# Expert outputs summed into the tokens' rows in memory, tile by tile, in a decoder block's sparse expert stage

## The reference

```python
xb = x + cross_attention(...)            # "after_cross"
x1 = self_attention(norm(xb)) + xn       # "x1"
h  = rmsnorm(x1) * ln2
s  = sigmoid(h @ router_w)               # 8 experts
top2 = argtop2(s + router_bias)          # ties: the lower expert
w  = s[top2] / sum(s[top2])              # the two shares
y  = sum over the two: w_e * ((silu(h @ wg[e]) * (h @ wu[e])) @ wd[e])
out = xb + x1 + y
```

## Time and profile before

| | us |
|---|---|
| median of 3 runs (3554.36 to 3559.09) | 3554.7 |
| the profiled execution | 3556.26 |
| its span, first to last instruction | 3554.5 |
| PE, DVE, ACT, POOL busy in the span | 3236.8, 2161.2, 1898.1, 1598.7 |
| granted TensorE clock, mean | 0.966 |
| expert block, from 3209.4 | 345.1 |

### The profile page before, as it was taken

The page is one execution under the profiler, slowest core; times in us unless marked ns, Lnnn a source line. Parts: engine busy times, 40 slices in busy tenths (PEclk is TensorE's granted clock), DMA queues, the critical chain, the costliest instruction groups (busy, mean ns, idle before and its releaser), DMA issues. The chain is left out here.

```text
span 3554.5 us, 61087 instructions
## 1 busy us (share of the span) xinstructions
PE 3236.8 (91%) x19346; PEld 2592.7 (73%) x19346; DVE 2161.2 (61%) x4705; ACT 1898.1 (53%) x4656; POOL 1598.7 (45%) x3082
## 2 busy tenths in 40 slices
PE   6799999999999999999899789799979999994992
PEld 3688888888888888888788455588857777772441
DVE  5476767677767676767553688654455756752223
ACT  3567676777676767676421477544353635531110
POOL 2677777777777777777330010255531010102103
PEclk8799999999999999999999899999989999997996
DMA  4122222222222222222342344333342021208325
GB/s 115 54 62 73 58 66 64 72 60 74 61 61 64 71 64 70 66 70 63 111 149 70 134 146 147 128 114 100 107 166 79 28 97 48 72 19 292 119 89 163
DMA packets 439368, 325.54 MB, mean 92 GB/s; under 512 B 131057, under 2 KB 348401, under 8 KB 438033
## 3 DMA queue, kind: packets, MB, share of 16 engines
q1 hardware_dynamic: 434064, 306.75, 29.0%
q0 software_dynamic: 5120, 16.78, 1.5%
HBM read 190.43 MB, written 133.04 MB: 91 GB/s over the span
## 5 line engine op out<-in xcount | busy, mean ns | idle before, releaser
L634 PE MATMUL gd_PJ<-xn_lead,gd_w_rest 128*128 128x512 f32 x1024 | 421.6, 412 | 0.0
L634 PE MATMUL gd_PJ<-xn_lead,gd_w_lead 128*128 128x512 f32 x1024 | 403.3, 394 | 0.0
L634 PE MATMUL gd_PJ<-xn_rest,gd_w_lead 128*128 128x512 f32 x1024 | 401.8, 392 | 0.0
L1076 POOL TENSOR_TENSOR gd_T<-gd_T,gd_prod 32x14 f32<-32x14 f32 (+6 forms) x896 | 312.5, 349 | 70.2
L1073 POOL TENSOR_TENSOR gd_prod<-gd_L,gd_T 32x14 f32<-32x14 f32 (+6 forms) x896 | 285.2, 318 | 70.2
L799 DVE SCALAR_TENSOR_TENSOR gd_conv<-gd_pre,gd_cur_a,gd_conv 128x512 f32<-128x512 f32 x384 | 300.5, 783 | 9.3 <-ACT gd_conv L957 2.4
L634 PEld LDWEIGHTS gd_PJ<-xn_lead,gd_w_lead 128*128 128x128 f32 x1024 | 193.6, 189 | 43.7
L634 PEld LDWEIGHTS gd_PJ<-xn_lead,gd_w_rest 128*128 128x128 f32 x1024 | 194.4, 190 | 37.4
L634 PEld LDWEIGHTS gd_PJ<-xn_rest,gd_w_lead 128*128 128x128 f32 x1024 | 194.6, 190 | 35.2
L2486 ACT ACTIVATE sa_E<-sa_B,sa_nmax 128x512 f32<-128x512 f32 (+3 forms) x256 | 131.4, 525 | 130.5 <-DVE sa_nmax L2602 130.5
L932 DVE SCALAR_TENSOR_TENSOR gd_og<-gd_B,ptab,gd_gate 128x512 f32<-128x512 f32 x64 | 48.0, 751 | 248.1 <-PE gd_B L648 248.1
(11 more groups left out here) (449 smaller groups left out, 8861.7 us busy)
## 6 DMA issues: line engine op xcount, KB each, us to landing
expert_rows<-xt_blank SPq DMA_DIRECT2D x16, 2048.0 KB, 7.5
turned_queries_keys<-f_wq SPq DMA_DIRECT2D x16, 1280.0 KB, 6.0
x_wo<-decay_sums SPq DMA_DIRECT2D x64, 256.0 KB, 3.9
triangles<-gd_Lo SPq DMA_DIRECT2D x64, 256.0 KB, 3.5
gd_W<-turned_image SPq DMA_DIRECT2D x64, 256.0 KB, 2.9
gd_T<-inverse_image SPq DMA_DIRECT2D x64, 256.0 KB, 3.4
gated_outputs<-gd_og SPq DMA_DIRECT2D x64, 256.0 KB, 2.8
go_ogt<-gated_outputs SPq DMA_DIRECT2D x16, 1024.0 KB, 5.9
```

The lines of the kernel that those rows point to most:

```text
L634: mm = pe.matmul(bank, w_parts[wp][:, j, k, :], rhs, start=(k == 0 and wp == 1), stop=(k == KT - 1 and wp + xp == 0))
L1076: nc.gpsimd.tensor_tensor(T16[:, rows, 0:j], T16[:, rows, 0:j], prod[:, rows, 0:j], ALU.subtract).then_inc(solving, 1)
```

## The change

Every row that travels to an expert gets 16 more floats (rows of 2112 bytes): the token's number, its first choice and its two shares. Behind the 16384 rows, 128 more are cleared, and all cleared rows carry numbers of 128 spare rows of the output sums. The shares are worked out with the routing (`shares`, eight small DVE operations on a batch), one step h after the second pick, and picks, places and rows come one to two steps h earlier than before.

A new memory tensor `sums` takes xb + x1. For batches 0 to 2 this is done in the middle of the next batch's heads: SP loads `after_cross` tiles into the two `hT` buffers, POOL adds them to `x1` in place, SP stores the result, and only then loads the next residual. For the last batch it is done in the expert block: SP issues four loads of `after_cross` behind the weights and ahead of the first expert tile, POOL adds, SP stores. The store of `x1` at each batch's end, the reload of `x1` and of all of `after_cross`, `slots`, the gathers, the additions of the last part and the 16 stores to `out` are gone.

In the expert loop DVE works out each tile's weight from what came with its rows (`weigh`, three small operations), ACT scales `y` by it on the way out of PSUM, and POOL adds the tile into `sums` by an indirect DMA that accumulates. POOL issues the one for tile j only when that for tile j - 1 has landed. `xr` has six buffers; SP reloads one when the accumulation of the tile in it has landed. After the last accumulation SP copies `sums` to `out`, memory to memory, in four transfers of 1 MB. The core of the diff:

```diff
-            slots()
-            shares()
+            shares(nc, then, R, last)
@@ self_attention, SP
+                    load_base(r, 0)
+                    load_base(r, 1)
+                    for i in range(CH):
+                        sp.wait_ge(base_added, r * CH + i + 1)
+                        sp.dma_start(acc_dram[bass.ds(r * SEQ + i * P, P), :], xt[:, i, :]).then_inc(R.base_out, 16)
+                        if i + 2 < CH:
+                            load_base(r, i + 2)
+                    sp.wait_ge(R.base_out, (r + 1) * CH * 16)
+                    load_residual(b)
-                for i in range(CH):
-                    sp.wait_ge(x1_ready, b * CH + i + 1 + CH)
-                    sp.dma_start(x1_dram[bass.ds(b * SEQ + i * P, P), :], xt[:, i, :]).then_inc(R.x1_out, 16)
@@ moe_sparse, SP
+            for i in range(CH):
+                sp.dma_start(xb[:, i, :], xb_dram[(last * CH + i) * P:(last * CH + i + 1) * P, :]).then_inc(xb_in, 16)
             load(0)
             load(1)
+            for i in range(CH):
+                sp.wait_ge(base_added, i + 1)
+                sp.dma_start(acc_dram[(last * CH + i) * P:(last * CH + i + 1) * P, :], R.x1[:, i, :]).then_inc(R.base_out, 16)
+            for j in range(2, MT):
+                sp.wait_ge(xr_turned, j - 1)
+                load(j)                                           # from j = 6: also summed >= 16 * (j - 5)
+            sp.wait_ge(summed, 16 * MT)
+            for b in range(B):
+                sp.dma_start(out_dram[b * SEQ:(b + 1) * SEQ, :], acc_dram[b * SEQ:(b + 1) * SEQ, :]).then_inc(out_done, 16)
@@ moe_sparse, POOL
+            pool.wait_ge(xb_in, 16 * CH)
+            for i in range(CH):
+                nc.gpsimd.tensor_tensor(R.x1[:, i, :], R.x1[:, i, :], xb[:, i, :], ALU.add).then_inc(base_added, 1)
+            pool.wait_ge(R.base_out, 16 * TILES)
+            for j in range(MT):
+                if j > 0:
+                    pool.wait_ge(summed, 16 * j)
+                pool.wait_ge(y_ready, j + 1)
+                rows = xr[:, j % SLOTS, AT_ID:AT_ID + 1].bitcast(I32)
+                nc.gpsimd.indirect_dma_start(acc_dram, bass.IndirectOffsetOnAxis(rows, 0), y[:, j % 2, :], None, compute_op=ALU.add).then_inc(summed, 16)
@@ moe_sparse, ACT, move_out(j)
+                act.wait_ge(weighted, j + 1)
                 if j >= 2:
-                    act.wait_ge(y_out[j % 2], j // 2 * 16)
-                nc.scalar.copy(y[:, j % 2, :], psY[j % 2][:, :]).then_inc(y_ready, 1)
+                    act.wait_ge(summed, 16 * (j - 1))
+                nc.scalar.activation(y[:, j % 2, :], psY[j % 2][:, :], ACT.Copy, scale=weight[:, j:j + 1]).then_inc(y_ready, 1)
@@ moe_sparse, DVE, between the gate product of tile j and the turned product of tile j - 1
+                weigh(j)
```

More of the change, by code:

```diff
@@ L2241, in drop_expert, with shares @@
     then(nc.vector.tensor_tensor(R.key[:], R.key[:], R.eq[:], ALU.add))
+def shares(nc, then, R, r):
+    for turn in range(2):
+        then(nc.vector.tensor_tensor(R.eq[:], R.pick[:, turn, R.tiles(r), :], R.sig[:, R.tiles(r), :], ALU.mult))
+        then(nc.vector.tensor_reduce(R.row[:, turn, :], R.eq[:], AX.X, ALU.add))
+    then(nc.vector.tensor_tensor(R.total[:, :], R.row[:, 0, :], R.row[:, 1, :], ALU.add))
+    then(nc.vector.reciprocal(R.total[:, :], R.total[:, :]))
+    for turn in range(2):
+        then(nc.vector.tensor_tensor(R.extra(AT_SHARE + turn), R.row[:, turn, :], R.total[:, :], ALU.mult))
 def places(nc, then, R, r, totals, within):
@@ L2979, in owners, with weigh @@
                 nc.vector.tensor_copy(row_i[:, :], row[:, :]).then_inc(owned, 1)
[L2981 to L2996 removed]
+                then(nc.vector.tensor_scalar(owner_key[:, :], owner[:, :], -1.0, float(EXPERTS), ALU.mult, ALU.add))
+            def weigh(j):
+                at = xr[:, j % SLOTS]
+                for turn, same in enumerate((ALU.is_equal, ALU.not_equal)):
+                    then(nc.vector.scalar_tensor_tensor(out=part[:, j, turn:turn + 1], in0=at[:, AT_FIRST:AT_FIRST + 1], scalar=owner_key[:, j:j + 1],
+                                                        in1=at[:, AT_SHARE + turn:AT_SHARE + turn + 1], op0=same, op1=ALU.mult))
+                nc.vector.tensor_tensor(weight[:, j:j + 1], part[:, j, 0:1], part[:, j, 1:2], ALU.add).then_inc(weighted, 1)
             for i in range(CH):
@@ L3037, in _ @@
             copy_products(MT - 1)
-            for t in range(TILES):
-                dve.wait_ge(added, t + 1)
-                dve.wait_ge(g_in[t % 2], t // 2 * 32 + 32)
-                nc.vector.scalar_tensor_tensor(out=x1[:, t, :], in0=got[:, t % 2, 0, :], scalar=share[:, 0, t:t + 1], in1=x1[:, t, :],
-                                               op0=ALU.mult, op1=ALU.add).then_inc(first_done, 1)
-                dve.wait_ge(first_done, t + 1)
-                nc.vector.scalar_tensor_tensor(out=x1[:, t, :], in0=got[:, t % 2, 1, :], scalar=share[:, 1, t:t + 1], in1=x1[:, t, :],
-                                               op0=ALU.mult, op1=ALU.add).then_inc(second_done, 1)
 def projections(nc, ctx):
```

194 lines of the change are left out of this document (81 added, 113 removed).

## The result

| | before | changed |
|---|---|---|
| time, median of 4 runs each | 3555.4 us (3554.4 to 3559.1) | 3519.0 us (3518.2 to 3520.4) |
| ratio | 1 | 0.9896, 95% interval 0.9879 to 0.9913 |
| profiled execution: time, span | 3556.3, 3554.5 | 3520.4, 3518.6 |

The changed kernel takes 36 us less; in a second set of runs 3517.05 against 3556.7, ratio 0.9892 (0.9877 to 0.9907). The forecast was 42 us less, 3513. The spans differ by 35.9 us; the rest of this text accounts for the 6.1 us between that and 42.0.

What follows compares the result with a forecast made beforehand. PE was taken to bound the expert loop (5.81 us a tile), a gather-add latency loop the end. Span terms 3494.3 + 0.3 + 16.0 + 1.4 + 0.5 = 3512.5, 42.0 less, so about 3513 us; 8-in-10 range 3506 to 3543.

Steps and rivals of the forecast that it cites:

- self-attention block: Barrier before the expert block: rows ready two routing steps of 2.72 us sooner, so POOL ends 5.4 us earlier.
- rows of tile 0 (T0): Expert block's first weight load to tile 0's first turn: four `after_cross` loads ahead on SP add 2.8 us.
- tile 2's wait: Expert block's start: with the 4 MB of `x1` gone, tile 2's 0.88 us wait for its transfer disappears.
- last output tiles to SP's release: Loop's tail: last three accumulations run one behind another at 4.8 us each, then 0.3 for SP's release.
- copy and end: Kernel's end: 4.19 MB copied memory to memory in 16 us, then 1.4 us to the end of the span.
- clearing: End of the cross-attention block: clearing longer rows, only the last store could show; taken as 0.5 us.
- the second of the two cases it named: Barrier before the expert block: POOL's longer way through it still comes last; gain 5.4 us, against 4.0 if DVE is last.
- Cost 0: Heads of batches 1 to 3: POOL's twelve base additions, 1.26 us each, and their loads and stores hide in POOL's waits.
- R: Expert loop: accumulation's round from POOL's release to the next release, taken as 4.8 us, under PE's 5.81 per tile.
- Rival B: Expert loop: accumulation's round of 6.80 us or more sets the pace, slower than before, 3558.5 to 3586; chance 0.14.
- rival A: Expert loop: accumulation's round becomes the pace, 39 us per us, but still faster, 3516 to 3553; chance 0.13.
- rival C: Copy at the end: reads and writes follow each other, 24.4 us instead of 16, span 3521; chance 0.14.

Runs made afterwards that it cites:

- e2: Changed kernel with the routing's steps put back to their old, later places; 3521.0 us, beside 3554.0 for the kernel before.
- e1: Changed kernel with POOL's twelve base additions in batches 1 to 3 doing only 8 of 512 columns; 3513.0 us, beside 3554.0 for the kernel before.
- e6: Changed kernel with the last batch's four `after_cross` loads issued behind the loads of tiles 0 and 1; 3515.4 us, beside 3557.5 before.
- e11: e9 plus 26 unread PE matmuls between the router's last matmul and the first tile's rows; 3493.2 us, ratio 0.9829 to the kernel before.
- e9: Changed kernel accumulating into the output, base added by accumulating DMAs, the last four held until tiles 0 and 1 landed; 3496.6 us, ratio 0.9834 to before.
- e4: Changed kernel with an unused 128x512 POOL addition ahead of each accumulation, lengthening its round; 3537.7 us, beside 3554.0 for the kernel before.
- e3: Changed kernel with each expert tile's indirect DMA writing plainly instead of accumulating; 3512.8 us, beside 3554.0 for the kernel before.
- e8: Changed kernel accumulating straight into the output, spare rows dropped by bounds, no final copy; 3503.1 us, ratio 0.9844 to the kernel before.
- e7: Changed kernel with cross-attention's result written into `sums` and `x1` added by accumulating DMAs, without POOL's additions; 3518.0 us, ratio 0.9887 to before.
- e5: Changed kernel with six unread matmuls on PE at the expert block's start; 3516.6 us, beside 3557.5 for the kernel before.

## Why the prediction was right, and where it was off

| step | forecast | measured |
|---|---|---|
| up to the self-attention block | 0 | +0.4 |
| self-attention block | -5.4 | -2.0 |
| rows of tile 0 (T0) | +2.8 | +2.6 |
| tile 0's group at the lower clock | 0 | +1.4 |
| tile 2's wait | -0.9 | -1.1 |
| last output tiles to SP's release | 14.4 + 0.3 | 16.25 |
| copy and end | 16.0 + 1.4 | 17.6 |
| clearing | +0.5 | 0 |

**The barrier: its mechanism held, one term was left out.** The prediction took 5.4 for the routing's earlier steps; e2 gives 5.2, and POOL is still last at the barrier, the second of the two cases it named. "Cost 0" for the base additions failed. Their cover was named as POOL's own waits, and on POOL they did hide; but they slowed DVE, which is on the batch's path, by 3.4 to 3.6 us in all (e1). An engine's idle time covers its own work, not what that work does to its neighbour.

**The start.** The loads ahead of tile 0 were forecast at 2.8, and T0 came 2.6 later, but the match is partly luck. e6 gives only 1.3 to 1.8 of it back. The other 1 us is the router, which ran at a granted clock of 0.50 (3.42 and 3.56 us, before 1.85 and 2.06): with the loads gone, T0 is 44.7 and 44.8 where the router is slow (e6, e11) and 43.8, like the kernel before, where it is fast (e9). The prediction had said of the clock at the start that nothing changes. Tile 2's wait for its transfer went as forecast. Missed was that tile 0's group can run wholly at a clock of 0.5 (6.70 against 5.32); it does so in some profiles of the same kernel and not in others (59.6 and 61.5 for G2), and whether it belongs to the change is open.

**The loop.** Right: 5.81 us a tile, and the accumulations hidden. R is 4.7 on the mean in e4, 4.7 to 5.65 where the rounds follow each other at the end of the changed kernel. The prediction's parts were 0.5 + 3.0 + 1.3; e3 shows them as 3.0 for a whole plain round, and 1.7 to 2.6 for the addition, of which 0.6 is POOL's issue. The 4.8 was a choice between 3.0 and 6.9 for which no row had the addition's price, so its closeness is in part luck. Rival B is ruled out, rival A was not far: two rounds in the loop, 6.08 and 6.19, were above the pace, and by the code it is the second buffer of `y` that lets them pass.

The Trainium skill's rule that an addition costs only a second read (Collectives: The Full Stack, "The bandwidth ceiling: the fold count and why AG ≠ RS ≠ AR", as told in the prediction) made R 3.9 and the time on the DMA engines 1.4 us. Both were too low here: an accumulation held the engines for 2.0 us against 0.69 of a plain write, POOL for 1.55 against 0.96, and it landed after 5.0 us instead of 2.7.

**The tail.** Three rounds of 15.2 instead of 14.4, and 1.0 of waiting for the fourth last. In the last tile PE waits 2.5 us for DVE, the granted clock falls to 0.50 about a microsecond after it starts again, and eight down matmuls take 5.4 us; the forecast did not see that, and it costs nothing, since the accumulations are later still (the last tile is out at 3492.9, its accumulation starts at 3496.26).

**The copy.** 17.6 with its end against 17.4, of which 15.5 are the transfers (16.0 forecast) and 2.1 the end (1.4 forecast); rival C (24.4) is out. The 16 was chosen between bounds of 13.4 and 24.4 without a row for such a transfer. e8 agrees: without the copy the span ends 15.2 us sooner behind the last issue.

The Trainium skill's figure of 358 GB/s for a core (DMA: Bandwidth & Descriptors, "Where 436 GB/s comes from"), read as both directions together, made it 23.4. Measured are 8.4 MB in 15.5 us, by estimate some 540 GB/s, so that reading of the figure does not hold here.

**The clearing.** Nothing: the last store is issued at 2254.08 and the next block begins at 2264.91, the same distance as in the earlier trace rows. The page's row of DMA issues (KB each, median us to landing), beside 7.5 us in the earlier trace rows:

```profile
expert_rows<-xt_blank SPq DMA_DIRECT2D x16, 2112.0 KB, 7.3
```

So the time was forecast 6 us too low, 0.2%, within its range. More than half of it is the one cost put at nothing, POOL's additions beside DVE (the block's term is off by 3.4 us); the rest is tile 0's group at the lower clock and the tail's rounds. The terms of the last part, which carried the gain, were off by less than 2 us. One slip of addition changes nothing: by the prediction's own parts the chances are 0.84 for faster and 0.13 for slower, not 0.83 and 0.14.

## What to carry to other kernels

When a serial chain of gather, add, gather becomes an accumulation in memory, ask two numbers first: the round of one accumulation, measured from issue to issue, and the time in which the compute makes a tile. If the first is smaller, it all hides but for the last few rounds; a second output buffer lets single longer rounds pass (here 6.19 us against 5.81). Price work that moves onto an idle engine by what it does to its neighbours as well, and look at the copy at the end: if the destination can be the output itself, the largest remaining piece is gone.

## What the runs showed that was not expected

- An accumulating indirect DMA costs its issuing engine 1.55 us, a plain one 0.96, and lands after 5.0 us instead of 2.7 (256 KB, 128 rows). By estimate it occupies the 16 DMA engines for 2.0 us instead of 0.69.
- POOL's 128x512 additions (1.27 us) stretch four 128x128 `tensor_scalar` on DVE from 1.27 to 2.35 us.
- An accumulation all of whose rows are out of bounds moves 0.00 MB; it lands after 2.7 instead of 4.7 us, and the round is 3.5 instead of 4.7 us (e8).
- The router's matmuls ran at a granted clock of 0.50 when PE had been idle for 8.4 us before the first turns (seven profiles), and mostly at 1.00 when it had been idle for 14.2 or 13.8 (before, e2); after 8.9 us both occurred (1.00 from early on in e9 and later in e7, 0.50 throughout in e11). Work ahead of them (e5) brought the clock up. What decides it without such work stays open.
